# Three hand-ordered work lists of a one-core vision tower rewritten, and one patch load moved ahead of a block of broadcasts

## The reference

```python
h = einsum('bnk,ok->bno', patches(x), W_tok)            # 256 -> 192
h = concatenate([cls_tok, h], axis=1)                   # 37 tokens
y = layernorm(h)
# mixing: k, v, sr from a layer norm of y; two scans over the tokens, one in each direction
a, b, m = e1*a + e2*v, e1*b + e2, max(m + decay, k)     # per token, per channel
y1 = y + (sr * (ef*af + eb*ab + ec*v) / (ef*bf + eb*bb + ec)) @ Wo.T
y2 = y1 + sigmoid(ln(y1) @ Wr_f.T) * (relu(ln(y1) @ Wk_f.T)**2 @ Wv_f.T)
h = h + y2
# experts: router with 4 groups of 4, best 2 groups, best 4 experts, weights normalised
c = route(layernorm(h))                                 # [token, 16]
moe = sum_e c[:, e] * ((silu(x @ gWg[e]) * (x @ gWu[e])) @ gWd[e])   # 16 experts, inner size 96
shared = (silu(x @ sWg) * (x @ sWu)) @ sWd
h = h + moe + shared
```

## Time and profile before

| | |
|---|---|
| median of 3 runs | 256.36 us (255.82 to 257.47) |
| the profiled execution | 256.1 us, of which its span is 254.0 us |
| PE busy | 241.0 us, 95% of the span |
| DVE busy | 191.3 us, 75% |
| ACT busy | 150.8 us, 59% |
| POOL busy | 17.9 us, 7% |
| granted TensorE clock | 0.999 of full |
| DMA | 17.46 MB, mean 69 GB/s |

### The profile page before, as it was taken

One profiled execution on the slowest core, in us unless ns is written; L12 is line 12 of the kernel. 1 busy time (PEld: TensorE's weight loads), 2 busy tenths in 40 slices (PEclk: granted clock), 3 DMA queues, 4 the chain that ended last, 5 costly groups with the idle time before them and its releaser, 6 DMA issues.

```text
span 254.0 us, 4370 instructions
## 1 busy us (share of the span) xinstructions
PE 241.0 (95%) x1508; PEld 220.9 (87%) x1508; DVE 191.3 (75%) x490; ACT 150.8 (59%) x311; POOL 17.9 (7%) x29
## 2 busy tenths in 40 slices
PE   8789789899999999999999999999999999999994
PEld 6676367677588898999999999999999999999993
DVE  5489988999989999999797799877423275854542
ACT  2698979978769998754776961436531442132220
POOL 6100302003101000101100001010000010000000
PEclk9999999999999999999999999999999999999999
DMA  6957290000000341000005510000254000015410
GB/s 170 321 199 294 86 283 22 0 3 0 0 3 13 100 102 44 0 3 0 1 6 153 177 59 1 1 3 0 73 174 138 25 3 0 1 36 100 100 32 27
DMA packets 13165, 17.46 MB, mean 69 GB/s; under 512 B 2359, under 2 KB 11224, under 8 KB 13016
## 3 DMA queue, kind: packets, MB, share of 16 engines
q1 hardware_dynamic: 12872, 17.08, 22.2%
q10 hardware_dynamic: 272, 0.11, 0.2%
HBM read 16.20 MB, written 0.99 MB: 68 GB/s over the span
## 4 chain that ended last, share of the span: by engine, by line
PE 67%; DVE 5%; SPq 5%; ACT 4%; issue 3%; DMA 2%; DVEq 0%
PE PG L978 17%; PE PA L998 17%; PE PG L980 11%; PE PF L998 6%; SPq L343 5%; PE PQ L978 3%; PE PX L1029 2%; PE PQ L980 2%; PE PG L1149 1%; PE PG L1148 1%; DMA pat<-in_patches 1%; PE PF L1013 1%; PE PF L988 1%; DVE stack L692 1%; PE PX L978 1%
## 5 line engine op out<-in xcount | busy, mean ns | idle before, releaser
L584 ACT ACTIVATE act<-PG,columns 128x222 f32<-128x222 f32 (+3 forms) x56 | 28.4, 507 | 58.5 <-PE PG L980 55.1
L978 PE MATMUL PG<-stack,hi_egu 128*128 128x222 f32 (+1 forms) x288 | 62.2, 324 | 0.0
L927 DVE SCALAR_TENSOR_TENSOR hid<-PG,columns,act 128x222 f32<-128x222 f32 (+1 forms) x52 | 27.2, 524 | 29.5 <-PE PG L980 25.0
L998 PE MATMUL PA<-w_ed,hid 128*124 128x192 f32 (+1 forms) x240 | 46.2, 327 | 0.3 <-DVE hid L936 0.3
L978 PEld LDWEIGHTS PG<-stack,hi_egu 128*128 128x128 f32 x288 | 45.6, 190 | 0.7 <-DVE hid L927 0.2
L980 PE MATMUL PG<-stack,lo_egu 128*128 128x222 f32 (+1 forms) x192 | 42.7, 304 | 0.0
L998 PEld LDWEIGHTS PA<-w_ed,hid 128*124 128x124 f32 (+1 forms) x240 | 38.6, 183 | 0.9 <-DVE hid L936 0.8
L980 PEld LDWEIGHTS PG<-stack,lo_egu 128*128 128x128 f32 x192 | 31.8, 190 | 0.0
L396 POOL TENSOR_TENSOR rstd<-var,minus_half 112x2 f32<-112x2 f32 (+3 forms) x12 | 13.9, 1156 | 187.6 <-DVE var L671 187.6
L998 PE MATMUL PF<-w_down,mix_hid 128*124 128x192 f32 (+1 forms) x120 | 22.8, 326 | 0.0
L936 DVE TENSOR_TENSOR hid<-hid,gates 128x222 f32<-128x222 f32 (+1 forms) x48 | 21.9, 461 | 0.9
(11 more groups left out here) (248 smaller groups left out, 441.9 us busy)
## 6 DMA issues: line engine op xcount, KB each, us to landing
gates<-in_w_egu SPq DMA_DIRECT2D x6, 512.0 KB, 5.1
gates<-c_rows SPq DMA_DIRECT2D x16, 138.8 KB, 2.8
gates<-c_rows SPq DMA_DIRECT2D x16, 92.5 KB, 2.8
gates<-c_rows SPq DMA_DIRECT2D x16, 83.2 KB, 2.6
w_ed<-in_w_ed SPq DMA_DIRECT2D x1, 1152.0 KB, 7.5
...
```

The source lines that it names most:

```text
L584: nc.scalar.activation(act[128 - gate:128, n % 2, 0:G.n], PG[0:gate, gate_bank(n), 0:G.n], ACT.Silu, bias=bias).then_inc(act_silu, 1)
L927: V_.scalar_tensor_tensor(out, PG[part, 1, 0:G.n], bias, act[part, i, 0:G.n], ALU.add, ALU.mult).then_inc(mul_done, 1)
L978: mm(out, w_hi[:, slot, cols], x[:, p, 0:G.n], start=(p == 0), stop=False, skip_group_check=True)
L998: last = mm(tile_out(P, G, t), src[:, G.ts[t]:G.ts[t] + G.tp], w, start=start and t != 1, stop=stop, skip_group_check=True)
```

## The change

Two things. On SP, `patches(3)` is issued ahead of the 24 broadcasts of group 0 and no longer behind them. And the three lists are written anew; the same steps with the same waits, interleaved in another way.

```diff
             patches(2)
+            patches(3)
             gates_across(0)
-            patches(3)
             gates_across(1)
...
 PE_ORDER = _order(
...
-    "G0:g1 F2:k G0:v1 G0:g2 F2:kt G0:v2 G0:g3 F2:v D0:cT G0:v3 G0:g4 F2:rt D0:d1 M1:tr2 F2:r G0:v4 G0:g5 D0:d0 M1:rf M1:up0",
+    "G0:g1 F2:k G0:v1 F2:kt G0:g2 G0:v2 G0:g3 F2:v G0:v3 D0:cT D0:d1 F2:rt G0:g4 M1:tr2 G0:v4 F2:r G0:g5 D0:d0 F3:tok0",
...
```

## The result

The changed kernel takes 258.02 us (median of 22 executions, 255.84 to 258.46), the kernel before 256.53 beside it (22 executions). The ratio is 1.0038, 95% interval 1.0025 to 1.0051: it is slower, by a little. (The ratio is estimated from the single executions of both kernels and is not the quotient of the two medians, which is 1.0058.) Two of the executions of the kernel before took 483.31 and 618.76 us; without them its median is 256.4. Forecast were 254.5 us and a range up to 257.8.

What follows compares the result with a forecast made beforehand. DVE was taken to set the pace up to 112 us (4.65 us idle), with PE full behind it. The running shift ended at -1.8 us, set against the median of 256.36: 254.5 us, range 252.3 to 257.8.

Steps and rivals of the forecast that it cites:

- Step 1: The start up to F0:o0: first layer norm some 0.85 us earlier, net 0 at scan0, shift -0.65 at F0:o0.
- Steps 2 and 3: F0:o0 to M0:tr3: shift -1.4 us at group 2's second embedding, then part given back, -0.8 at M0:tr3.
- Step 4: M0:tr3 to D0:cT: DVE's router ends 1.4 us earlier, shift -1.7 us at D0:cT.
- Step 5: F3:tok0 ahead of M1:rf: waits of some 0.65 us there and 0.75 at D0:d2, shift -1.07 at M1:up1.
- Step 6: M1:up1 to F2:o0: the 0.71 us wait at 97.31 and some 0.2 of small ones go, shift -2.0.
- Step 7: Behind 112 us: nothing won, four tight places, 0.2 us in all for near misses, shift -1.8 at the end.
- (b): ACT's four added table loads, 5.1 us: 0.25 us to spare at G1:g7; taken as 0, at most 5 us.
- (c): DVE waits longer for F3:w0, but PE needs S1:s5 only 1 us later; taken as 0.
- (d): F3:o0 late: chain to M3:tr2 takes 6.2 us while PE has 6.2 us of steps; taken as 0.
- rival 1: Behind 112 us the gain is given back in waits for DVE and ACT chains: 256.4 us, chance 0.19.
- rival 3: Table loads make ACT the bound in the front of group 3, 4.9 us on top: 259.4 us, chance 0.12.
- rival 4: Each of the four added table loads holds ACT twice as long, 5.1 us more: 264.5 us, chance 0.01.

Runs made afterwards that it cites:

- b3_patches_only: Kernel before with only patches(3) issued ahead of the 24 broadcasts, all lists as before: 255.64 us, ratio 0.9962.
- b2_old_to_68: Kernel before with the changed lists only behind M0:tr3 and the patches of group 3 moved ahead: 255.86 us, ratio 0.9975.
- a2_low_k_back: Changed kernel with DVE's first thirteen steps as before (W:k ahead of F0:stats1, W:v behind F0:var1): 256.07 us, ratio 0.9981.
- c1_free_root: b3_patches_only with the low halves of k and v behind F0:ln1 on DVE: 255.17 us, ratio 0.9956.
- d2_new_lists_free_root: Changed kernel with only W:k and W:v moved behind F0:ln1 on DVE: 256.02 us, ratio 0.9988.
- b4_fill_spins: Changed kernel with three more spins (useless matmuls) in PE's waits ahead of F0:v and F0:r: 256.08 us, ratio 0.9991.
- e1_w_first_again: Changed kernel with F0:w1 directly behind W:sgu and F0:w2 directly behind W:egu0 on ACT, a repeat run: 256.62 us, one execution.
- b1_exps_early: Changed kernel with the old start (ACT to F0:w2, DVE to F0:top1) and F1:exps ahead of F2:tok0 on ACT: 256.23 us, ratio 0.9992.
- c2_scan1_first: b3_patches_only with M0:ln2 behind F1:scan1 on DVE and F1:rt ahead of M0:ln2 on ACT: 255.78 us, ratio 0.9975.

## Why the prediction was wrong, point by point

The landmarks of the prediction on PE, in work done (us; "more ahead" is the length of steps that stand ahead of the landmark only in the new list):

| landmark | before | changed | more ahead | shift | forecast |
|---|---|---|---|---|---|
| F0:o0 | 34.40 | 35.96 | 1.09 | +0.47 | -0.65 |
| F2:tok1 | 45.34 | 46.69 | 1.09 | +0.26 | -1.4 |
| M0:tr3 | 67.85 | 69.99 | 0 | +2.14 | -0.8 |
| D0:cT | 78.73 | 80.78 | 0.56 | +1.49 | -1.7 |
| M1:up1 | 89.17 | 92.32 | 1.50 | +1.65 | -1.07 |
| F2:o0 | 112.77 | 114.96 | 1.11 | +1.08 | -2.0 |
| D3:d13 | 249.76 | 250.97 | 0 | +1.21 | -1.8 |

The first two rows look better than they are: PE has low halves done ahead of time there, which fill its waits, while DVE is 1.56 us behind (F0:z at 35.05 against 33.49). Behind M0:tr3 the sum is right: I had -1.0 from there to the end, and it is 1.21 - 2.14 = -0.93. In part this is luck. Stretch by stretch it is -0.65, +0.16, -0.57 and +0.13, where I had -0.9, +0.63, -0.93 and +0.2, so errors of up to 0.47 cancel. And 0.71 of the 0.93 is the DMA alone (181.91 us from M0:tr3 to D3:d13 before, 181.20 in b3_patches_only). b2_old_to_68, which reaches M0:tr3 0.51 us sooner behind F0:top1 than a2_low_k_back does, needs 181.35 from there, against 180.98 in a2_low_k_back and in the changed kernel. So part of what the new lists seem to win behind M0:tr3 is probably what they lost ahead of it. Up to M0:tr3 I had -0.8 and it is +2.14. The 2.94 us between are three pieces.

**Step 1, the start: 1.37 us.** F0:top1 should have come 0.87 early and came 0.50 late. This is the step that failed first. The statistics moved up by 0.42, not 0.85, because they are bound by the embedding. The root behind them, for which I had kept the length of before, adds 0.71 to F0:ln1 (3.13 against 2.42). And 0.21 remain of the steps now ahead of F0:top1 (ACT's two copies, F1:aggr1) less F1:stats1, which now stands in DVE's wait: 14.24 in a2_low_k_back, where the root is as before, against 14.03. I had taken the cover of the low half of k for free because no engine waits for it; it ran beside POOL's root and held it. a2_low_k_back, c1_free_root and d2_new_lists_free_root show it.

**The clock: 1.15 us.** No step of the prediction has it, so it was put at nothing without a reason; I wrote only that the clock was 1.00. Step 1 priced the wait of F0:kt at 0.6 on the path and did not ask what PE's idle time there does to PE. b4_fill_spins shows that in this kernel the low clock comes of these waits: with spins in them 0 of 12 executions have it instead of 17 of 22. It does not come in every execution. The delay then goes by way of F0:sub0 and F0:w1 to DVE, at a place where the new ACT list has three weight conversions ahead of F0:w1; of the 1.15 us, 0.40 are left when they stand behind (e1_w_first_again, one profile).

**Steps 2 and 3, from F0:top1 to M0:tr3: 0.42 us.** At full clock (a2_low_k_back) this stretch takes 46.82 us against 46.33 before, +0.49, where I had +0.07. The 0.52 of the wait at M0:ln2 are won as forecast, and two waits of DVE, 0.20 at F1:ab00 and 0.18 for ACT's R, go as well; ACT hands back 0.71 at F1:sa and 0.22 at M0:tr2b. So DVE's waits come to 0.93 instead of 0.90, and DVE's M0:ln3 comes 45.39 us behind F0:top1 instead of 45.15. The other 0.25 are lost on ACT behind it, at a step that I had overlooked: the new list has the low half of egu5a ahead of M0:ln3. First the kernel before, then a2_low_k_back:

```profile
66.81 0.99 ACT L422 ACTIVATE norm<-h,shift,rstd 112x192 f32<-112x192 f32 x2
...
67.29 0.60 ACT L414 ACTIVATE lo_egu<-PA 128x512 fp32r<-128x512 f32 x1
67.91 0.98 ACT L422 ACTIVATE norm<-h,shift,rstd 112x192 f32<-112x192 f32 x2
```

DVE's M0:ln3 starts at 66.67 and 67.52, so ACT follows 0.14 and 0.39 us behind it. I had said that DVE sets the pace here; b1_exps_early and c2_scan1_first show that ACT is level with it between 40 and 50 us: there both swaps moved DVE's holes and did not close them.

**Step 4:** -0.65 from M0:tr3 to D0:cT where I had -0.9, right in kind. **Step 5:** the wait of F3:tok0 for F2:r is 0.61 booked (0.65 forecast), that of D0:d2 (0.75 forecast) does not exist. **Step 6:** the wait for the patches is gone, worth 0.70 by b3_patches_only (0.71 forecast), and -0.57 of the -0.93 for the whole step appear. **Step 7:** +0.13 against +0.2, with one wait of PE that the kernel before does not have:

```profile
124.10 0.76 PE L978 MATMUL PG<-stack,hi_sgu 128*128 128x370 f32 x3 [0.25 <-DVE hid L927]
```

All twelve loads take 1.28. Eleven are followed within 0.14 us, the first of all, at 1.77, by a wait for a DMA. The one that was to be tight:

```profile
146.25 1.28 ACT L584 ACT_TABLE_LOAD   x1
147.54 0.57 ACT L584 ACTIVATE act<-PG,columns 128x370 f32<-128x370 f32 x1
```

ACT is busy 16.43 of 20.00 us from 138 to 158 (12.51 in the earlier trace rows) and PE waits nowhere there. The tight places (b) to (d) and rivals 1, 3 and 4 did not occur. With rival 4 goes the price on the page ScalarE: Activation LUTs of the Trainium skill, section What ACT_TABLE_LOAD costs: the 1380 ns of drain that it gives show at none of these loads.

The range missed by 0.2 us, and it missed because all rivals that end slower stood behind 112 us, on ACT. The start, with its serial chain over four engines, had none.

**What the new lists are worth.** From F0:top1 to the end at full clock they take 227.80 us, against 228.24 before and 227.54 with the DMA alone. So they gain 0.44 with the DMA, and without it they would lose 0.26; this is a difference, no run has the new lists with the DMA at its old place.
